# Rotary cross attention over 32 examples: both halves of a score group as one TensorE step, the turning of keys in three steps, and another order of the frame

## The reference, cut to what matters

```python
q = split_heads(query @ Wq.T)          # 16 heads of 16 features, 112 tokens
k = split_heads(key @ Wk.T)            # key = value = the context, 375 rows
v = split_heads(value @ Wv.T)
q = _apply_rope(q)
k = _apply_rope(k)
logits = jnp.einsum('bhqd,bhkd->bhqk', q, k) * scale
attn = jax.nn.softmax(logits, axis=-1)
out = jnp.einsum('bhqk,bhkd->bhqd', attn, v)
out = out.transpose(0, 2, 1, 3).reshape(b, t, d)
return out @ Wo.T + bo
```

## Time and profile before

| | |
|---|---|
| median of 3 runs | 3127.98 us (3122.63 to 3129.04) |
| profiled execution, its own time | 3129.71 us |
| its span, first to last instruction | 3127.9 us |
| PE busy over the span | 2765.3 us (88%) |
| DVE, ACT, POOL busy | 2251.7, 1662.0, 960.0 us |
| granted TensorE clock, mean | 0.942 of full |
| the stage of the change | from about 1700 to about 2415 us |

### The profile page before, as it was taken

How to read it: one execution, slowest core, us unless ns; L and a number is a source line. 1 busy time by engine, 2 the same in 40 slices (tenths; PEclk the granted TensorE clock), 3 DMA queues, 4 the chain that set the end, 5 groups by cost and what they waited for, 6 DMA issues and landing times. The chain is left out here.

```text
span 3127.9 us, 75474 instructions
## 1 busy us (share of the span) xinstructions
PE 2765.3 (88%) x28144; PEld 2019.4 (65%) x28144; DVE 2251.7 (72%) x5782; ACT 1662.0 (53%) x3243; POOL 960.0 (31%) x1219
## 2 busy tenths in 40 slices
PE   7998999999999999667998799999997999983980
PEld 6887566666666665556886466666664777763970
DVE  5997567777777776557887577767763899984656
ACT  4776555555555555343554244444443788862540
POOL 0000344555555555450000100000000135546771
PEclk9999999999999999688999799999998999995995
DMA  7940445545545544362000233333330877866768
GB/s 180 281 121 6 134 132 158 158 132 157 165 134 150 167 139 134 95 199 69 2 2 8 60 73 72 72 70 73 73 63 22 237 229 234 248 178 203 222 195 255
DMA packets 364853, 414.63 MB, mean 133 GB/s; under 512 B 108016, under 2 KB 330512, under 8 KB 364368
## 3 DMA queue, kind: packets, MB, share of 16 engines
q1 hardware_dynamic: 218176, 220.63, 26.7%
q10 hardware_dynamic: 127216, 139.94, 15.9%
q0 software_dynamic: 19104, 49.22, 4.6%
HBM read 125.33 MB, written 252.45 MB: 121 GB/s over the span
## 5 line engine op out<-in xcount | busy, mean ns | idle before, releaser
L814 POOL TENSOR_TENSOR x_rstd<-x_var,g_minus_half 112x1 f32<-112x1 f32 x128 | 74.6, 583 | 708.0 <-DVE x_var L810 707.4
L2190 DVE TENSOR_REDUCE x_top<-x_scores 112x2 f32<-112x750 f32 x256 | 228.3, 933 | 79.2 <-PE x_scores L2034 78.2
L1369 ACT ACTIVATE x_probs<-x_held,x_minus_top 112x488 f32<-112x488 f32 x256 | 177.7, 697 | 173.2 <-DVE x_minus_top L1425 173.2
L1242 POOL TENSOR_TENSOR x_probs<-x_probs,x_inverse 112x488 f32<-112x488 f32 x256 | 250.4, 998 | 10.2
L1283 PE MATMUL x_ring<-w_xkv,x_kv 128*122 128x512 f32 x512 | 236.3, 594 | 0.0
L1276 PE MATMUL x_ring<-x_kv,w_xkv 128*128 128x488 f32 x512 | 232.9, 588 | 1.1 <-ACT x_kv L1345 1.1
L932 ACT ACTIVATE x_v<-x_ring 122x512 f32<-122x512 f32 (+1 forms) x224 | 113.1, 505 | 182.9 <-PE x_ring L1283 152.0
L2137 ACT ACTIVATE x_probsT<-x_scores 125x1792 f32<-125x1792 f32 x96 | 159.7, 1664 | 81.9 <-PE x_scores L2052 81.9
L1419 DVE SCALAR_TENSOR_TENSOR x_held<-x_scores,x_keep 112x976 f32<-112x976 f32 x128 | 150.4, 1175 | 73.4 <-PE x_scores L1296 51.7
L814 POOL TENSOR_TENSOR a_rstd<-a_var,g_minus_half 112x1 f32<-112x1 f32 x64 | 35.3, 551 | 525.1 <-DVE a_var L810 525.1
L1237 POOL TENSOR_TENSOR x_inverse<-x_sums,x_minus_one 112x2 f32<-112x2 f32 x128 | 89.6, 700 | 227.0 <-ACT x_probs L1369 227.0
(11 more groups left out here) (471 smaller groups left out, 7360.8 us busy)
## 6 DMA issues: line engine op xcount, KB each, us to landing
expert_slots<-d_empty ACTq DMA_DIRECT2D x32, 3612.0 KB, 17.1
by_position<-r_by_position SPq DMA_DIRECT2D x64, 784.0 KB
first_slots<-d_empty SPq DMA_DIRECT2D x8, 3612.0 KB, 33.8
r_bias<-by_position SPq DMA_DIRECT2D x64, 392.0 KB
m_rows<-expert_slots SPq DMA_DIRECT2D x143, 129.0 KB, 2.7
x_kq_swapped<-x_kq_raw ACTq DMA_DIRECT2D x64, 243.5 KB, 3.6
x_slots<-x_kq SPq DMA_DIRECT2D x512, 30.4 KB
m_rows<-expert_replies SPq DMA_DIRECT2D x32, 448.0 KB, 8.4
```

Of the source, the lines that this page charges most:

```text
L1242: self.nc.gpsimd.tensor_tensor(probs, probs, self.inverse[0:T, u:u + 1].to_broadcast([T, XK]), ALU.mult).then_inc(self.weighted, 1)
L1369: nc.scalar.activation(self.probs[u % 6][0:T, :], self.held[m % 2][0:T, i, :], ACT.Exp, scale=self.scale, bias=self.minus_top[0:T, m % 2, ...
L2190: nc.vector.tensor_reduce(self.top[0:T, g, 2 * half:2 * half + 2], self.scores[0:T, at:at + 1024].rearrange("t (a c) -> t a c", c=512)[:, ...
```

## The change

The three pairs of banks are dealt out anew, and the plan has another order. On PE a name `h` now does both halves of its group, `h` first, after waiting for both pairs; the names `g` remain as steps of DVE alone. The DVE step `rope` is cut in three at its wait: `rope` (cosine product), `swap` (the wait and the sine product) and `sum`, with other steps between them. The number of instructions of each kind is the same.

```diff
-        self.plan = Flow(2, [("h0", 3), ("g0", 3), ("headsB", 5), ("tr0", 4), ("g1", 3), ("q", 1), ("back0", 5),
-                             ("tr1", 4), ("k1", 1), ("k0", 1), ("stats", 0), ("scale", 0), ("back1", 5), ("h1", 3),
-                             ("g2", 3), ("onT", 5), ("rope", 1), ("v0", 2), ("ctx0", 0), ("tr2", 4), ("v1", 2),
-                             ("xT", 0), ("h2", 3), ("g3", 3), ("h3", 3), ("ctx1", 0), ("headsA", 4), ("v2", 2),
-                             ("project", 5), ("put", 3)],
+        self.plan = Flow(2, [("h0", 3), ("g0", 3), ("headsB", 5), ("stats", 0), ("tr0", 4), ("q", 1), ("k1", 1), ("scale", 0),
+                             ("h1", 3), ("g1", 3), ("k0", 1), ("back0", 5), ("tr1", 4), ("rope", 1), ("v0", 2), ("back1", 5),
+                             ("swap", 1), ("h2", 3), ("g2", 3), ("v1", 2), ("ctx0", 0), ("onT", 5), ("sum", 1), ("tr2", 4),
+                             ("xT", 0), ("v2", 2), ("h3", 3), ("g3", 3), ("ctx1", 0), ("headsA", 4), ("project", 5), ("put", 3)],
...
-        self.first_pair = {"g0": 0, "g1": 0, "g2": 2, "g3": 1, "h0": 1, "h1": 0, "h2": 2, "h3": 0,
-                           "tr0": 1, "tr1": 0, "tr2": 0}
+        self.first_pair = {"h0": 0, "g0": 2, "tr0": 0, "h1": 2, "g1": 0, "tr1": 1, "h2": 0, "g2": 2, "tr2": 0,
+                           "h3": 2, "g3": 1}
...
-        elif name == "rope":
+        elif name == "sum":
             pool.wait_ge(self.turned, b + 1)
...
-        if name in ("g0", "g1", "g2", "g3", "h0", "h1", "h2", "h3"):
-
-            g, half = int(name[1]), "gh".index(name[0])
-            if name == self.score_names[[n[0] in "gh" for n in self.score_names].index(True)]:
+        if name in ("h0", "h1", "h2", "h3"):
+
+            g = int(name[1])
+            if g == 0:
                 pe.wait_ge(self.slotted, 256 * (b + 1))
                 self.tiles_set_up(pe, b)
-            self.bank_free(pe, name, b)
-            for a in range(2 * half, 2 * half + 2):
...
+            self.bank_free(pe, f"h{g}", b)
+            self.bank_free(pe, f"g{g}", b)
+            for half in (1, 0):
+                for a in range(2 * half, 2 * half + 2):
...
             nc.vector.tensor_tensor(self.kq_part[:], self.kq_raw[:], bc(const("cosX"), 1, DC), ALU.mult)
+        elif name == "swap":
             dve.wait_ge(self.swapped, 32 * (b + 1))
             at_least(dve, self.slotted, 256 * b)
             chain.link(nc.vector.tensor_tensor(self.kq[:], self.kq_swapped[:], bc(const("sinX"), 1, DC), ALU.mult))
+        elif name == "sum":
             nc.vector.tensor_tensor(self.kq[:], self.kq[:], self.kq_part[:], ALU.add).then_inc(self.turned, 1)
```

More of the change, by code:

```diff
@@ L1921, in __init__ @@
         super().__init__(nc, G, W)
-        self.plan = Flow(2, [("h0", 3), ("g0", 3), ("headsB", 5), ("tr0", 4), ("g1", 3), ("q", 1), ("back0", 5),
[3 rows of a table removed]
-                             ("project", 5), ("put", 3)],
-                         bankless=("tr0", "tr1", "tr2", "g0", "h0", "g1", "h1", "g2", "h2", "g3", "h3", "rope", "stats", "scale"),
+        self.plan = Flow(2, [("h0", 3), ("g0", 3), ("headsB", 5), ("stats", 0), ("tr0", 4), ("q", 1), ("k1", 1), ("scale", 0),
[3 rows of a table added]
+                         bankless=("tr0", "tr1", "tr2", "g0", "h0", "g1", "h1", "g2", "h2", "g3", "h3", "rope", "swap", "sum",
+                                   "stats", "scale"),
                          ahead=8, behind=5, turns=3, unroll=12)
-        self.first_pair = {"g0": 0, "g1": 0, "g2": 2, "g3": 1, "h0": 1, "h1": 0, "h2": 2, "h3": 0,
-                           "tr0": 1, "tr1": 0, "tr2": 0}
+        self.first_pair = {"h0": 0, "g0": 2, "tr0": 0, "h1": 2, "g1": 0, "tr1": 1, "h2": 0, "g2": 2, "tr2": 0,
+                           "h3": 2, "g3": 1}
         names = [name for name in self.plan.names if name in self.first_pair]
@@ L2023, in pe @@
         slots = self.slots[par]
-        if name in ("g0", "g1", "g2", "g3", "h0", "h1", "h2", "h3"):
-            g, half = int(name[1]), "gh".index(name[0])
-            if name == self.score_names[[n[0] in "gh" for n in self.score_names].index(True)]:
+        if name in ("h0", "h1", "h2", "h3"):
+            g = int(name[1])
+            if g == 0:
                 pe.wait_ge(self.slotted, 256 * (b + 1))
                 self.tiles_set_up(pe, b)
-            self.bank_free(pe, name, b)
-            for a in range(2 * half, 2 * half + 2):
[L2032 to L2036, removed]
+            self.bank_free(pe, f"h{g}", b)
+            self.bank_free(pe, f"g{g}", b)
+            for half in (1, 0):
+                for a in range(2 * half, 2 * half + 2):
+                    slot = slice(SLOT * a, SLOT * (a + 1))
+                    at = 512 * (2 * self.first_pair["gh"[half] + name[1]] + a % 2)
+                    ins = nc.tensor.matmul(self.scores[0:T, at:at + S2], slots[slot, g, S2:KQ], slots[slot, g, 0:S2],
+                                           start=True, stop=True)
+                ins.then_inc(self.scored[half], 1)
         elif name == "put":
```

## The result

| | before | changed |
|---|---|---|
| median | 3128.51 us of 4 runs (3122.63 to 3129.45) | 3199.55 us of 4 runs (3193.51 to 3205.39) |
| ratio, with its 95% interval | 1 | 1.0232 (1.0211 to 1.0253) |
| profiled execution, its span | 3129.71, 3127.9 us | 3204.43, 3202.5 us |
| a frame on time, `put` to `put` | 19.4 us | 21.6 us |
| last residual add of the stage | 2406.68 us | 2471.55 us |

The changed kernel is slower by 2.3%. The forecast was 3181 us with a range of 3150 to 3225, so the direction and the mechanism held and the size was 18.6 us short. (Of the eleven executions of the kernel before that stand beside experiments 9 and 10, two disturbed ones, at 3661 and 4087 us, are left out of the ratios.)

What follows compares the result with a forecast made beforehand. TensorE was taken to set the old pace; after the change, a chain through the exchange makes frames 21.28 us instead of 19.37. 27 frames give 51.6 us, fill and drain 2: 3181 us, range 3150 to 3225.

Steps and rivals of the forecast that it cites:

- TensorE's saving: Score halves on PE: four pairs save 0.51 us per frame, 0.10 given back after `tr0`; TensorE alone would need 18.96 us.
- The chain: Through the frame, from `h0` via exchange, sine product, maximum of `h2`, `tr2` and `h3` to `put`: 21.28 us.
- The waits: PE waits about 1.1 us before `h2`, 0.56 before `h3`, 0.3 to 1 before `tr2`, none before `put`.
- The sum: Whole kernel: 1.91 us more per frame gives 51.6 us over 27 frames, plus 2 for fill and drain.
- Lateness: Late exchanged keys cost PE the same before and after, nearly one for one, so it cancels.
- Fill and drain: Both ends of the stage, where latencies already rule: put at 2 us, between 0 and 9.5.
- The rival of the clock (0.12): TensorE's clock falls behind PE's new waits: 3209 us if in a third of frames, 3265 if in every; chance 0.12.
- The rival that TensorE makes up for its waits (0.10): Steps behind each PE wait get shorter, as weight loads and dispatch run ahead: faster, 3115 us; chance 0.10.
- The covered chain (0.04): Broken at the exchange, half the price covered: a frame of 19.4 to 19.6 us, 3128 to 3134; chance 0.04.
- That the pairing does nothing: The four score slots don't overlap, 0.5 us lost: +10, 3191 us; counted inside the forecast, no chance of its own.
- the later placement: Placement's 16 transfers after `sum` end 7.4 us into the next frame, before the exchange at 8.4: no cost.

Runs made afterwards that it cites:

- experiment 9: New frame order and bank dealing, half waits, exchange as its own step, cosine product behind `xT`, against the kernel before: 3114.14 us, ratio 0.9948.
- experiment 10: The kernel of experiment 9 with both halves waiting for both pairs again: 3117.14 us, ratio 0.9956 to the kernel before.
- experiment 1: The changed kernel with `swap` moved behind the maxima of `h2` and `g2` on DVE: 3166.70 us, ratio 1.0119 to the kernel before.
- experiment 4: The changed kernel with `swap` behind the maxima of `h2` and `g2` and the exchange issued behind `v0`: 3151.54 us, ratio 1.0077 to the kernel before.
- experiment 2: The changed kernel with the exchange issued later, behind the copy of `v0`, `swap` still ahead of the maxima: 3283.99 us, ratio 1.0499 to the kernel before.
- experiment 7: The kernel before with only `rope` split: `swap` stays where `rope` was, `sum` goes behind `h3`: 3156.72 us, ratio 1.0081.
- experiment 3: The changed kernel with each half waiting for its own pair of banks only: 3186.53 us, ratio 1.0182 to the kernel before.
- experiment 8: The changed kernel with `swap` behind `g2` and each half waiting for its own pair only: 3158.94 us, ratio 1.0075 to the kernel before.
- experiment 6: Different frame order and bank dealing with the double wait, exchange as its own step, `sum` behind `g3`, against the kernel before: 3126.46 us, ratio 0.9982.

## Why the prediction was right in kind and short in size

**TensorE's saving.** Four pairs side by side at 0.83 each: the four stretches of 0.90 busy are there, and 0.83 from start to start (1940.12 to 1940.95). That price held. Of the net saving of 0.41 us little is left, though: the frame of 21.62 less its four waits (0.99, 0.15, 0.67, 0.56) is 19.25, against a forecast of 18.96 and 19.37 before. This doesn't enter the time, as the chain sets the frame.

**The chain.** From `h0` to the end of `k0` 7.74 us against a forecast of 7.62; to the exchange 0.77 (0.76); to the sine product 4.17 (4.17); to its end 1.17; then 0.12 before the maxima start; to `tr2` 0.99 (1.0); to `h3` 2.93 (2.91); to the end of `put` 3.73 (3.65). That makes 21.62 against 21.28. The 0.34 us missing are, but for a few hundredths, in three small terms:
- 0.11: the two key steps take 1.37 each (1938.75 to 1940.12, 1940.95 to 1942.32), where I took 1.31 and 1.32 from two that follow each other. Each of them now has `h1`, a step of 32 rows, as a neighbour. The rows of experiment 9 show the price: a key step between two transposes takes 1.26 us to the next start (2011.38 to 2012.64), and one right behind the 32-row `tr1` takes 1.37 (2014.03 to 2015.40). I had weighed such a change for `tr0` alone, which takes 1.08 (1936.69 to 1937.77) instead of 0.97. So each change between 32-row steps and others costs some 0.1 us. The old frame has six stretches of 32-row steps, not five as I counted, and the new one seven: one more, paid at both ends, about 0.2 us where I gave back 0.10. The Trainium skill (TensorEngine Tiling (Array Packing), Key Properties) says that a change of the tiling mode drains TensorE; these rows agree.
- 0.12: DVE's pause from the end of the sine product (1948.43) to the next maximum (1948.55), which I left out.
- 0.09: `project` takes 0.95 (1955.06 to 1956.01) instead of 0.86, with no `v2` ahead of it.

Over 27 frames the 0.34 are 9.2 us, half of what the forecast lacked.

**The waits.** Before `h2` 0.99 (forecast 1.1), before `h3` 0.56 (0.56), before `tr2` 0.67 on time and 1.86 late (0.3 to 1), before `put` none (none). The wait at `h2` is indeed inside the other: experiment 1 takes the product out of the way, and the frame falls to 20.89, not to the old 19.37. Then the exponentials set it, as experiment 4 shows.

**The sum, its failed terms.** The last residual add of the stage moved by 64.9 us; I had 51.6 for the frames and 2 for the ends. 9.2 of the 11.3 missing are the 0.34 above. The rest is small and has both signs. Lateness, which I let cancel, adds up to some 12.7 us after and 9.3 before (each `put` distance above 21.62, or above 19.38, without the first two frames and that of the longest wait), and the frame of the longest wait grew by 2.7. Fill and drain, which I put at 2, came out a little below nothing: the first `put` comes 7.1 us earlier, and from the last `put` to the residual add it is 3.9 us longer. The other rest lies outside the stage: the span grew by 74.6 us, 9.7 more than the stage; in the medians, 71.0 us apart, about 6 of these remain. They are in phases that the change doesn't touch, and in all likelihood scatter between executions: from the last residual add to the end it is 721.2 us before and 731.0 in the changed kernel, and in the ten other kernels, which have these phases unchanged too, between 721.6 and 728.8. The two traces compared here happen to be the ends of that range. So the missing size is the 0.34 us in the chain, a few microseconds of lateness, and this luck.

**The rival of the clock (0.12).** Partly true. In four late frames the granted clock fell behind a wait of 1.5 to 1.9 us (0.57 from 1906 to 1910), but in another one, with 1.85, it did not, nor behind the three waits of a frame on time, of about 1 us at most. (Its fifth fall is at the stage's longest wait, as in the earlier trace rows.) In experiment 2, with waits of 3 us in every frame, it fell in every one. It is a surcharge on lateness here, of about 1.0 us in a frame where it comes, some 4 us in all. The Trainium skill (TensorE: Matmul & The Clock Gate, A second HAM failure mode: psum-queue depth-cycling) had named short idles at PSUM banks; the waits of up to 1 us in every frame of the changed kernel leave its clock alone.

**The rival that TensorE makes up for its waits (0.10).** False: the steps behind the waits of a frame on time are as long as before (0.90, 1.14, 0.90). **The covered chain (0.04):** false on time. **That the pairing does nothing:** the two halves of each stretch overlap, so it does what it says.

**An assumption next to the sum.** I costed the later placement at nothing. In the changed kernel that holds, as `sum` comes before `tr2`. Experiment 7 shows how near the edge it is: a few microseconds later, and the next sine product waits.

## What to carry to other kernels

Where an engine works through a written order, look for the instruction that waits for a transfer and count who stands behind it: one place in DVE's order was worth 1.1% here, and it costs no instruction to move. Merging two steps that wait for different things was cheap where the order left each of them room (0.15 us a frame in experiment 10); the room needed can be added up from the trace before, in this kernel 2.9 us behind each `tr`. When part of a sequence is moved later, follow its output to the next use of the same buffer, even a frame on (experiment 7).

## What the runs showed of the hardware, unexpected

- A half group alone can last as long as two side by side: 0.89 us against 0.90, and 0.82 to the next step, where the kernel before had halves at 0.72. So idle time won by starting one half earlier came back as duration (experiments 3 and 8). Why it isn't 0.72 there was not tried.
- Issuing a transfer from ACT costs it nothing while an activation is still running: 0.47 us at 2012.49 inside an exponential until 2013.06. Ahead of it, both issues took 1.12 us in which it started nothing.
- The length of a single wait alone did not tell whether TensorE's granted clock would fall to its lower level of 1.2 GHz. In the changed kernel it fell behind waits of 1.52, 1.69, 1.86 and 1.90 us and stayed up behind 1.31 and 1.85; it stayed up behind 1.70 in experiment 1 and behind 1.90 in experiment 3, where it fell 20 us later at a wait of 0.86. Behind the waits of about 3 us of experiment 2 it fell every time.
- A change between 32-row steps and others cost TensorE about 0.1 us: a key step took 1.37 us next to a 32-row step and 1.26 between two transposes (experiment 9).
- The exchange landed in 3.1, 3.9 and 5.3 us (least, median, longest) in experiment 6, where it runs beside placement, against 2.9, 3.6 and 4.9 in the changed kernel. In experiment 7, also beside placement, the median is 3.7, so placement's part in this is not shown.
